# GpSimd waits for the landing of a tile's indirect DMAs in a routed vision layer: gathers and input scatters, not the scatters of combined rows

## The reference

```python
h = h + attn(layernorm(h))                   # 12 heads, within an image
x = layernorm(h)                             # 2368 tokens x 192
w_fk = topk_sparsify(softmax(x @ W_fk ... ), 4)   # 4 of 128 "feature" experts per token
w_rk = topk_sparsify(softmax(x @ W_rk ... ), 4)   # 4 of 128 "restore" experts per token
hid = einsum('bsnr,bsn->bsr', einsum('bsd,ndr->bsnr', x, f_know), w_fk)    # 192 -> 128
out = einsum('bsnd,bsn->bsd', einsum('bsr,nrd->bsnd', hid, r_know), w_rk)  # 128 -> 192
h = h + out
```

## Time and profile before

| | |
|---|---|
| time, median of 3 runs | 784.07 us (784.05 to 784.77) |
| profiled execution, span | 1062.3 us |
| PE / DVE / ACT / GpSimd busy in it | 583.6 / 387.7 / 339.6 / 403.1 us |
| mean granted TensorE clock | 0.749 |
| indirect DMAs | 76 input scatters, 152 gathers, 76 scatters of combined rows |

### The profile page before, as it was taken

The page is one execution under the profiler, slowest core; times in us unless marked ns, Lnnn a source line. Parts: engine busy times, 40 slices in busy tenths (PEclk is TensorE's granted clock), DMA queues, the critical chain, the costliest instruction groups (busy, mean ns, idle before and its releaser), DMA issues.

```text
span 1062.3 us, 16453 instructions
## 1 busy us (share of the span) xinstructions
PE 583.6 (55%) x5060; PEld 453.4 (43%) x5061; DVE 387.7 (36%) x1412; ACT 339.6 (32%) x738; POOL 403.1 (38%) x397
## 2 busy tenths in 40 slices
PE   7888998999863534298631115960410576217600
PEld 6677786787642313178510003760300265003500
DVE  3666887887884845290011110000111000330013
ACT  3445575657521330055300002530100353004400
POOL 4413443143135536500077770000677101770065
PEclk9699999998965656599855556985755698558955
DMA  5987768860941963267532223689722475335652
GB/s 139 358 349 261 277 256 346 321 276 18 174 96 63 192 155 108 77 178 196 141 95 64 66 74 83 180 237 282 208 76 63 125 221 157 100 91 171 183 148 76
DMA packets 163730, 177.44 MB, mean 167 GB/s; under 512 B 12777, under 2 KB 147218, under 8 KB 163666
## 3 DMA queue, kind: packets, MB, share of 16 engines
q1 hardware_dynamic: 150290, 149.20, 45.8%
q0 software_dynamic: 13376, 27.41, 8.8%
HBM read 76.55 MB, written 100.02 MB: 166 GB/s over the span
## 4 chain that ended last, share of the span: by engine, by line
PE 32%; issue 25%; another core or an unknown queue 12%; ACT 10%; DVE 9%; SPq 5%; DMA 4%; POOL 2%; ACTq 0%; POOLq 0%; DVEq 0%
PE bank L1139 8%; PE bank L855 5%; PE bank L1150 4%; PE bank L1124 4%; ACT qk_pad L1240 3%; PE bank L902 3%; POOL gat L712 2%; SPq L496 2%; PE bank L840 1%; DVE smax L1634 1%; PE bank L1157 1%; SPq L485 1%; PE bank L963 1%; ACT xsT L1416 1%
## 5 line engine op out<-in xcount | busy, mean ns | idle before, releaser
L712 POOL DMA_INDIRECT gat<-wide_dram,slots x152 | 146.3, 962 | 365.1 <-SPq L549 320.0
L1139 PE MATMUL bank<-matrices,xsT 96*32 96x128 f32 (+1 forms) x1536 | 98.9, 330 | 226.1 <-issue 174.9
L1407 ACT ACTIVATE os<-bank 128x256 f32<-128x256 f32 (+1 forms) x160 | 69.9, 438 | 384.5 <-remote 230.1
L1139 PEld LDWEIGHTS bank<-matrices,xsT 96*32 96x32 f32 (+1 forms) x1536 | 51.7, 120 | 263.7 <-issue 201.3
L1124 PE MATMUL bank<-ident,xs 128*96 128x128 f32 (+1 forms) x480 | 91.6, 300 | 59.4 <-issue 39.5
L1911 DVE TENSOR_SCALAR acc<-gat,wts 128x128 f32<-128x128 f32 x19 | 5.4, 286 | 311.6 <-DMA gat<-wide_dram,slots 191.7
L1416 ACT ACTIVATE xsT<-bank 96x512 f32<-96x512 f32 (+1 forms) x160 | 76.4, 487 | 91.9 <-PE bank L1124 53.7
L699 POOL DMA_INDIRECT wide_dram<-x2b,slots x76 | 75.2, 989 | 71.1 <-issue 38.8
L1150 PE MATMUL bank<-matrices,xsT 96*128 (+1 forms) x576 | 97.3, 308 | 2.6 <-ACT xsT L1416 2.3
L1124 PEld LDWEIGHTS bank<-ident,xs 128*96 128x96 f32 (+1 forms) x480 | 56.2, 139 | 90.3 <-issue 72.3
L656 POOL TENSOR_TENSOR qk_sum<-qk_pad 64x888 f32<-64x888 f32 x16 | 26.6, 1665 | 167.6 <-ACT qk_pad L1240 156.6
(11 more groups left out here) (187 smaller groups left out, 973.5 us busy)
## 6 DMA issues: line engine op xcount, KB each, us to landing
wide_dram<-zeros SPq DMA_DIRECT2D x6, 5632.0 KB, 19.5
mid_dram<-zeros SPq DMA_DIRECT2D x8, 2816.0 KB, 25.9
xs<-wide_dram SPq DMA_DIRECT2D x80, 192.0 KB
wide_dram<-os SPq DMA_DIRECT2D x80, 192.0 KB, 2.3
matrices<-in_L_ffn_f_know SPq DMA_DIRECT2D x8, 1536.0 KB
matrices<-in_L_ffn_r_know SPq DMA_DIRECT2D x8, 1536.0 KB, 11.8
wide_dram<-os SPq DMA_DIRECT2D x80, 128.0 KB, 2.6
xs<-mid_dram SPq DMA_DIRECT2D x80, 128.0 KB
```

The source lines that it names most:

```text
L712: pool.indirect_dma_start(gat[i][:, e, :], None, wide_dram[b], bass.IndirectOffsetOnAxis(ap=slots[:, t, k:k + 1], axis=0))\
L1139: last = pe.matmul(bank[2 + r][q * FIRST:(q + 1) * FIRST, k * width:(k + 1) * width], xsT[r % 2][0:kp, c:c + FIRST], matrices[0:kp, at:at ...
L1407: act.activation(os_[r][:, :, 0:width], bank[2 + r][:, 0:SB * width].rearrange("p (k w) -> p k w", w=width), ACT.Copy)\
```

## The change

GpSimd gets a wait, with its count-up, behind the four scatters of each tile of input rows, and one behind the four gathers of each tile, except those of layer 1 and batch 1. The scatters of combined rows get none.

```diff
                     pool.indirect_dma_start(wide_dram[b], ...x2b[:, t - BATCHES[b][0], :], None)\
                         .then_inc(scattered[min(t, BATCHES[0][1])], 16)
+                if b == 0:
+                    pool.wait_ge(scattered[t], 64)
+                else:
+                    pool.wait_ge(scattered[-1], 64 * (t - BATCHES[1][0] + 1))
+                take(pool)
...
                     pool.indirect_dma_start(gat[i][:, e, :], None, wide_dram[b], ...)\
                         .then_inc(gathered[layer][i], 16)
+                if layer == 0 or b == 0:
+                    pool.wait_ge(gathered[layer][i], 64 * (t // 2 + 1))
+                    take(pool)
```

## The result

The changed kernel takes 914.76 us, median of four runs (911.45 to 917.98), beside 784.42 for the kernel before: a ratio of 1.1655, 95% interval 1.1608 to 1.1702, or 130 us more. I had predicted 839, in a range of 785 to 870. The direction was right, the rise was 75 us short (130 where I had 55), and the time stands where the rival of the late landings put it, around 911.

What follows compares the result with a forecast made beforehand. GpSimd's chain of indirect DMAs was taken to gate phases 2 and 3. Waits of 1.8 us added 11.7 + 34.2 + 9.3 = 55 us to the median, forecasting 839 us, range 785 to 870.

Steps and rivals of the forecast that it cites:

- the rival of the late landings: Transfers under load land much later than in the profile, at twice the price of a wait: around 911 us, chance 0.04.
- the price of a wait: Each added GpSimd wait was taken to cost 1.8 us, between 1.3 and 2.1, with the top raised to 2.4.
- a sign that its size is off: Waits that read well under 1.3 or above 2.4 us in the profile after would show the size wrong.
- The heavier estimate: With HBM access of 2 us at high load a wait could cost 3.6 us: 127 us more, 911 in all.
- First scatters: Waits behind the first batch's input scatters: ten of 1.8 us, less 6 us spare before the second plan, 11.7 us late.
- Second scatters: Eight waits behind the second batch's input scatters, 14 us, priced at nothing because phase 0 covers them.
- Layer 0: Nineteen waits behind layer 0's gathers, no spare in the chain: 19.8 us at phase 2, 14.4 at phase 3, 34.2 together.
- Layer 1, first batch: Eleven waits behind these gathers, hidden behind phase 3 with 10.5 us to spare: last gathers start 9.3 us late.
- The 1062 us: The profile's span held 292 us of starvation, taken as almost absent from timed runs; without it the sum was 787 us.
- The rule on the trace's records: The block writing trace records holds its producers back: by it the timed sum is 787 us, without it near 1062.
- GpSimd has room: The 0.31 us between indirect DMAs may come from recording, so bursts fit under phase 1: 795 or 784 to 786, chance 0.14.
- Faster: Waits give PE pauses from real starvation by GpSimd's bursts: at most 14 us back, 770, or 777 with half; chance 0.14.

Runs made afterwards that it cites:

- the 784.6-us profile: The kernel before, unchanged, profiled once more: span 784.6 us, time of that run 786.34 us.
- half_gather: The kernel before with two of the four gathers of a tile in layer 0, the combine reading them twice: 766.05 us against 783.05.
- gat0_only: The kernel before with only the waits behind layer 0's gathers, none behind the scatters: 850.12 us against 781.04.
- fill_a: The kernel before, no waits, two memsets of a dead tile behind each tile's gathers (layer 0, layer 1's first batch): 852.69 us against 783.05.
- fill_b: The kernel before, no waits, four memsets of a dead tile behind each tile's gathers (layer 0, layer 1's first batch): 913.86 us against 783.05.
- r_behind: The changed kernel with its eight restore-matrix loads moved behind SP's wait for the first batch's combined rows: 911.06 us, ratio 1.1606 to before.

## Why the prediction was right and wrong

**The step that failed is the price of a wait.** "I take 1.8" of a range of 1.3 to 2.4. The pauses in layer 0 were 68.9 us in 17 rows at its scatters and two more at gathers; by the table above, 68.1 us over 19 tiles are 3.6 each, twice the 1.8 and above the 2.4, which the prediction had named as a sign that its size is off. The working went wrong twice.

First, in quiet stretches the pause was 2.3 to 3.0 us, 2.0 to 2.7 more than the 0.30 it replaces, so at the upper end of 1.3 to 2.1 and above. I had the two parts, the landing of 1.63 us and GpSimd's waking of 0.82; their sum of 2.45 is the pause of a quiet wait. I took less by supposing, with no row for it, that part of the waking lay in DVE's 1.63 already. The changed kernel shows both engines on one landing, a quiet one and then one under load; in each triple the last gather, DVE's combine and GpSimd's next DMA:

```profile
641.18 0.95 POOL L717 DMA_INDIRECT gat<-wide_dram,slots  x1 [0.30 <-issue]
643.81 0.29 DVE L1919 TENSOR_SCALAR acc<-gat,wts 128x128 f32<-128x128 f32 x1 [11.01 <-DMA gat<-wide_dram,slots]
644.72 1.02 POOL L728 DMA_INDIRECT mid_dram<-comb,slots  x1 [2.59 <-DMA gat<-wide_dram,slots]
...
568.08 0.95 POOL L717 DMA_INDIRECT gat<-wide_dram,slots  x1 [0.30 <-issue]
...
574.36 0.29 DVE L1919 TENSOR_SCALAR acc<-gat,wts 128x128 f32<-128x128 f32 x1 [14.67 <-DMA gat<-wide_dram,slots]
575.27 1.02 POOL L728 DMA_INDIRECT mid_dram<-comb,slots  x1 [6.24 <-DMA gat<-wide_dram,slots]
```

DVE starts 1.68 and 5.33 us behind the gather's end, GpSimd 0.91 behind DVE both times (0.77 to 0.96 at all thirty tiles): the waking comes on top, and only the landing grows with the load.

Second, the load. I let it raise the top to 2.4, from SP's stores, which land in 2.6 us at the median. But a median over 80 stores says little of the stretches with the most traffic, and the waits stand just there: three of the first batch's ten beside the feature matrices' load (share 1.14), three to four of eleven beside the restore matrices' (0.98), and those of phases 2 and 3 beside the expert rows (0.82 to 0.83). The rows that I leaned on the earlier trace rows had 73 to 146 GB/s because that execution was starved; the same bursts in the 784.6-us profile stand beside 250 to 267 GB/s:

```profile
468.85:584.74 115.89, 66.01 (x838) 56.95 (x839) 15.01 (x44) 34.21 (x72) 86.45 (x90) 0.75 0.90 267
673.70:736.30 62.60, 43.08 (x404) 28.72 (x404) 17.13 (x41) 28.74 (x72) 42.54 (x45) 0.91 0.85 250
```

I had seen that ("lighter than a timed run's would be"), and gave the late landings 0.04 all the same. With the load known to be heavier than in every row that gave the price, its upper end should have been open, and the rival's chance far higher. Of the two errors this one took the time out of the range: with the quiet pauses everywhere (2.3 us at the scatters, 2.6 at the gathers, less the 0.30 each and less the room found below) the three steps would be some 18, 44 and 19 us, an estimate of 865.

**The heavier estimate.** The Trainium skill (DMA: Bandwidth & Descriptors, Latency and other measured facts) gives 0.2 us for an access to HBM on average and 2 us at high load, from which the prediction had a wait of 3.6 us and 30 + 68 + 29 = 127. The runs gave 33, 68 and 28, and a mean of 3.6 in layer 0. The trace agrees with the sum; it does not show one high-load value, but pauses from 2.3 to above 7 whose mean happens to lie there. That the two meet within 4 us is in part luck, since part of the missing price was GpSimd's waking and the rooms were smaller than I had them.

**First scatters.** 11.7 predicted, 33.3 measured. The way was right: ten pauses, less the few us by which the second plan comes later than the scatters' landing. The ten sum to 39.3 us in the changed kernel, 36.3 less the 0.30 each that stood there before; seven are 2.3 to 2.5, and the three beside the feature matrices 7.1 to 8.7 (the row of the longest names DVE's `slots` as its releaser, but that tile's were written at 333.34, before the pause began). Without the waits the last of these scatters ends at 378.08 in the 784.6-us profile, with them at 413.28: 35.2 later, of which 33.3 reach SP's first load. So the room is about 2 us, not 6.

**Second scatters.** Nothing, as predicted: phase 0 with its wait on them became 1.5 us shorter.

**Layer 0.** 34.2 predicted, 68.1 measured: 19 pauses in full, as said, at twice the price. That GpSimd's chain has no spare there was right to a few us: from the first gather I had 113.7 us to phase 2's first load and 203.3 to the end of phase 2, against 115.9 and 196.7 + 8.5 = 205.2 in the 784.6-us profile. half_gather confirms it.

**Layer 1, first batch.** 9.3 predicted, 28.5 measured; eleven pauses over some 6 us of room rather than 10.5. The tail's burst is unchanged, as said: 40.4 us in the earlier trace rows, and 40.35 after the change, from 864.69 to the end of the last gather at 905.04.

**The 1062 us.** The subtraction of 292 us gave a sum of 787 that fits the median, and the steps built on it held. But its reason was wrong: not a recording, one odd execution. The rule on the trace's records (the Trainium skill, NOTIFIC — the notification-queue block, Overflow: three behaviours) has no run here to bear it out: 23 timed executions of before took 778 to 789 us, and one with a profile 786.

**The rivals.** GpSimd has room: out, by half_gather and by gat0_only. Faster: no stretch gained more than 1.5 us, and the fills, in which GpSimd issues no DMA for 2.9 or 4.9 us behind a tile, were not faster either. Late landings: right, to 4 us.

## What to carry to other kernels

A wait for an indirect DMA that was just issued cost its landing plus the waking of the engine that waits, the two added. The landing has to be read in the stretch where the wait will stand: look for the bulk loads (here two loads of matrices) that run beside it. Where an engine's chain sets the end, a pause of p us in n steps costs n x p, less the room (fill_a and fill_b), so a median taken elsewhere is multiplied by n as well. And where the only profile is unlike the timed runs, its durations under load can lie well below a timed run's: leave the top of the range open.

## What the runs showed of the hardware

The pause behind four indirect DMAs of a tile was 2.3 to 3.0 us at a DMA share of 0.17 to 0.29, 2.6 to 5.5 at 0.70 to 0.83, and 6.0 to 8.7 at 0.98 to 1.14. With the loads of restore matrices, in blocks of 1536 KB, it was 6.0 to 6.2, without them 2.6 at the same tiles, and r_behind moved both together. Whether the DMA engines or the memory behind them make the landing late, no run here separates. Of the pause, 0.77 to 0.96 us is GpSimd's start behind DVE's on the same landing; a wait for a landing that was over cost no idle time beyond the usual 0.30. For SP's own transfers the medians hide this: stores of products still land in 3.0 us at the median (2.6 before).

The first profile of before, with 292 us in which PE and DVE hardly ran, has no like among the other executions of that kernel. What held them stays open.
